# A graph network's message passing on one Trainium2 core: steps of eight tiles without loops, node spans of 32, and stores moved into the counting stage

## The chip, the cores and the metric

The kernel runs on one core of a Trainium2 chip as one program. The core has TensorE (PE, matmuls, with its weight loads PEld), VectorE (DVE), ScalarE (ACT), GpSimd (POOL) and SyncE (SP, which here only issues transfers). The time is the device time of the execution in microseconds, and the median of the runs counts.

## The reference

A graph has 3125 nodes with 96 features and 100,000 edges `src -> dst`, sorted by `dst`; each edge has four attributes. Four layers follow one another, each on `relu(layernorm(x))` and added to x: ten hops of a propagation, a softmax-weighted neighbour sum, message passing with an edge MLP, and two graph convolutions. Cut to the layer that the change is mostly about:

```python
def mlp(h, W, b, gamma, beta):
    h = relu(h @ W + b)
    mu = mean(h, axis=0); var = mean(square(h - mu), axis=0)
    return gamma * (h - mu) * rsqrt(var + EPS) + beta

node_feat = mlp(x, W_node, b_node, g_node, beta_node)             # 3125 x 96
edge_feat = mlp(edge_attr, W_edge, b_edge, g_edge, beta_edge)     # 100000 x 96
message = concatenate([x[src], x[dst], edge_feat], axis=1)        # 100000 x 288
message = mlp(message, W_msg, b_msg, g_msg, beta_msg)             # 100000 x 96
x = x + segment_sum(message, dst, num_segments=3125) + node_feat
```

The other layers need only, for each pair of nodes, how many edges join them: the kernel builds that table of counts once, as a dense matrix of 25 x 25 blocks of 128 x 128, and multiplies with it.

## The kernel before, in words

The stages run one after another, with a barrier between them. `setup` loads the indices, finds which windows of nodes each batch of edges touches, and splits attributes and edge weights into bf16 parts that are stored to HBM (`attr_parts`, `w_edge`); the `dst` of each step's edges is stored as 16 copies of a row (`dst_row`, L227). `count_edges` builds the counts by matmuls of one-hot matrices; beside them it runs the edge MLP once over all edges for its mean and variance. `propagate` does the ten hops, `gen_conv` the second layer. `prepare_messages` computes for each node what it gives to a message as source (`p_rows`, in HBM, for gathers) and as destination (`q`, kept in SBUF as three bf16 parts), and `pass_messages` does the rest; `finish_messages` normalizes; `gcn_first` and `gcn_second` follow.

In `pass_messages` (stage L1210 to L1480) the 784 tiles of 128 edges go in 196 steps of four (`STEP_TILES = 4`), in groups of 14 steps, the middle groups in a hardware loop. For each step:

- SP loads the attributes (L1248) and the `dst` row, broadcast to 128 partitions (L1253).
- POOL gathers the four tiles' rows of `p_rows` (L1276) into one of seven slots of `z`. A slot is free when the step seven before it has been squared (ACT) and summed (PE).
- PE multiplies the attributes with the edge weights (L1404), ACT rectifies (L1360), PE multiplies that with `w_part` (L1412, fp32).
- For each block of 128 nodes that the step's `dst` fall in (a "visit"; 220 in all) DVE makes a turned one-hot (L1288) and copies the block's `q` (L1290), and PE adds the destination's part (L1420, three products per tile).
- DVE adds the gathered rows (L1297), ACT rectifies (L1368) and squares (L1372), DVE adds the squares (L1316).
- For each visit again, DVE makes the one-hot of nodes (L1306, L1309), and PE sums the messages by node into a block of PSUM (L1436). PSUM holds all 25 blocks to the end of the stage.
- PE runs matmuls with zeros (L1393), two ahead of each step's sums and one behind, which add nothing to the sums.

How many visits a step has isn't known when the program is built. The engines read it from a table (L1187, `TENSOR_LOAD`), and the visits are hardware loops with registers as bounds: L1284 and L1303 on DVE, L1416 and L1430 on PE. Order within an engine is the order of the code; between engines it is set by semaphores, for instance

```python
pool.wait_ge(squared, s - SLOTS + 1)
pool.wait_ge(summed, s - SLOTS + 1)
```

ahead of a slot's next gathers.

## Time and profile before

| | us |
|---|---|
| median of 3 runs (3156.49 to 3165.76) | 3164.98 |
| the profiled execution | 3195.45 |
| its span, first to last instruction | 3193.7 |
| setup | 0 to 72 |
| counting, with the edge MLP's statistics | 75 to 649 |
| degrees, first layer norm | 649 to 682 |
| ten hops | 682 to 1218 |
| second layer | 1218 to 1390 |
| preparing messages | 1390 to 1488 |
| passing messages | 1488 to 2950 |
| finish, two convolutions | 2950 to 3193 |

The profile is of one execution; its own time is about 1% above the median, so what is read from it is compared with 3195.45 and carried over to the median at the end. A share of busy time over the whole span (PE 77%, DVE 45%, POOL 28%, ACT 26%) mixes stages with different limits, so the rows below are read by stage. "Idle before" is an engine's idle time directly ahead of an instruction, and the name behind the arrow is what ended it; `issue` is a wait for nothing that the profile shows. Rows with a `q` behind the engine (SPq, PEldq) are of its sequencer.

### The profile page before, as it was taken

The numbers are of one execution on the slowest core, as the hardware profiler recorded it, in microseconds if no ns is written. First come the engines' busy times: TensorE is split into PE (matmuls) and PEld (weight loads), VectorE is DVE, ScalarE is ACT, GpSimd is POOL, SyncE is SP. The second block draws the span as 40 slices with busy tenths as digits, with TensorE's granted clock in tenths as the row PEclk, the third lists the DMA queues.
The fourth block names the chain that finished last, engine by engine and source line by source line (L and its number), as shares of the span: only waits on it lengthen the run. The fifth ranks groups of instructions, "written<-read, shape, count | busy, mean of one in ns | idle before, by whom it ended". The sixth has DMA issues, their size and how long they took to land. (4 is left out here: it accounts for less than half of the span.)

```text
span 3193.7 us, 70454 instructions
## 1 busy us (share of the span) xinstructions
PE 2446.3 (77%) x18850; PEld 1853.2 (58%) x18851; DVE 1451.4 (45%) x3266; ACT 829.0 (26%) x1637; POOL 897.1 (28%) x1115
## 2 busy tenths in 40 slices
PE   0777777779999994965788778788777777777479
PEld 0333444479999993533555556556556655555357
DVE  4967766654444445453333333333333333333642
ACT  1585566521111111111222222222122212122110
POOL 2311211100000000002555555555544555552000
PEclk9989878779999996976677766776776666767799
DMA  5111111100000033001122112111111111111000
GB/s 172 31 46 44 48 55 54 60 27 2 2 2 2 2 131 143 1 10 31 50 58 56 50 51 55 52 52 51 49 48 47 50 45 48 47 49 29 2 1 16
DMA packets 92732, 141.30 MB, mean 44 GB/s; under 512 B 28596, under 2 KB 70916, under 8 KB 92526
## 3 DMA queue, kind: packets, MB, share of 16 engines
q1 hardware_dynamic: 67438, 100.16, 9.2%
q0 software_dynamic: 25088, 38.59, 5.1%
q8 instruction: 106, 1.74, 0.2%
q14 instruction: 100, 0.82, 0.1%
HBM read 105.31 MB, written 33.35 MB: 43 GB/s over the span
## 5 line engine op out<-in xcount | busy, mean ns | idle before, releaser
L1276 POOL DMA_INDIRECT e_z<-p_rows,rows x784 | 767.6, 979 | 653.1 <-issue 270.4
L844 PE MATMUL ps_hop<-y,counts 128*128 128x192 f16 x6250 | 525.1, 247 | 22.4 <-DVEq L768 11.1
L844 PEld LDWEIGHTS ps_hop<-y,counts 128*128 128x128 f16 x6250 | 520.0, 98 | 27.3 <-DVE y L796 11.3
L1436 PE MATMUL ps_e_seg<-e_z,e_hot 128*128 128x96 f32 x1760 | 352.1, 361 | 238.4 <-DVE e_hot L1309 144.2
L1436 PEld LDWEIGHTS ps_e_seg<-e_z,e_hot 128*128 128x128 f32 x1760 | 328.7, 269 | 346.9 <-issue 339.9
L553 PE MATMUL ps_counts<-hot_w,hot_p 128*128 x1196 | 295.9, 380 | 127.2 <-DVE hot_p L527 78.9
L527 DVE TENSOR_TENSOR hot_w<-iota_w,places_now 128x1600 f16<-128x1600 f16 x300 | 297.1, 990 | 205.7 <-PE ps_counts L553 167.4
L1368 ACT ACTIVATE e_z<-e_z 128x384 f32<-128x384 f32 x196 | 102.4, 523 | 1068.1 <-DVE e_z L1297 829.0
L1412 PE MATMUL ps_e_z<-w_part,e_u 96*128 96x96 f32 x1568 | 316.5, 365 | 4.1 <-issue 3.7
L1412 PEld LDWEIGHTS ps_e_z<-w_part,e_u 96*128 96x128 f32 x1568 | 275.5, 264 | 67.9 <-issue 67.3
L1393 PE MATMUL ps_e_seg<-e_zeros,ident_h 128*128 128x512 f16 x608 | 273.5, 516 | 17.8 <-issue 16.8
L553 PEld LDWEIGHTS ps_counts<-hot_w,hot_p 128*128 x1196 | 120.2, 104 | 266.5 <-issue 221.2
L1420 PE MATMUL ps_e_z<-e_q_now,e_hot_t 128*128 x2640 | 222.7, 249 | 48.4 <-issue 40.0
L1288 DVE TENSOR_SCALAR e_hot_t<-e_dst_rows,block_node 128x512 f16 x220 | 80.1, 364 | 369.7 <-issue 310.0
L1420 PEld LDWEIGHTS ps_e_z<-e_q_now,e_hot_t 128*128 x2640 | 203.4, 126 | 65.6 <-issue 60.3
L494 POOL TENSOR_TENSOR places_now<-places,origins (+1 forms) x302 | 110.2, 365 | 458.7 <-DVE hot_p L527 265.9
L1267 POOL MEMSET e_attr<- 39x1024 bf16 x1 | 0.9, 945 | 844.2 <-POOLq L1001 844.2
L1306 DVE TENSOR_SCALAR e_place<-dst_h,block_neg 128x4 f32 (+1 forms) x220 | 53.4, 243 | 348.4 <-PE ps_e_seg L1436 142.4
L826 ACT ACTIVATE y<-wide 128x96 f32 x250 | 70.7, 283 | 465.3 <-DVE wide L789 465.3
L1297 DVE TENSOR_TENSOR e_z<-ps_e_z,e_z 128x384 f32<-128x384 f32 x196 | 109.3, 558 | 169.9 <-remote 117.3
L1309 DVE TENSOR_TENSOR e_hot<-iota_p,e_place 128x512 f32<-128x512 f16 x220 | 152.6, 694 | 9.3 <-DVE e_place L1306 1.4
L617 ACT ACTIVATE attr_split<-ps_counts 128x400 f16<-128x400 f32 x200 | 100.6, 503 | 193.5 <-PE ps_counts L546 193.2
(307 smaller groups left out, 2635.4 us busy)
## 6 DMA issues: line engine op xcount, KB each, us to landing
e_dst_rows<-dst_row SPq DMA_DIRECT2D x196, 128.0 KB
count_rows<-attr_split SPq DMA_DIRECT2D x25, 800.0 KB, 3.7
counts<-count_rows SPq DMA_DIRECT2D x25, 800.0 KB, 6.8
e_z<-p_rows,rows POOLq DMA_INDIRECT x784
attr_parts<-attr_split SPq DMA_DIRECT2D x9, 784.0 KB, 8.9
e_attr<-attr_parts SPq DMA_DIRECT2D x196, 36.0 KB
attr<-attr_parts SPq DMA_DIRECT2D x50, 140.6 KB
dst_row<-counts SPq DMA_DIRECT2D x16, 196.0 KB
```

The lines of the kernel that those rows point to most:

```text
L494: nc.gpsimd.tensor_tensor(now[:, bass.ds(i & 3, 1), :, :, :].rearrange("p a j c t -> p (a j) c t"), k.places[:, bass.ds(tile, BATCH), :].u ...
L527: made = nc.vector.tensor_tensor(hot[:, s, :, :].rearrange("p j (e t) -> p j e t", t=2), iota_w[:, 0:n].rearrange("p (e t) -> p e t", t=2) ...
L553: mm = pe.matmul(ps[:, j % 2, 0:WIDE], hot_p[:, bass.ds(i & 1, 1), t, :].rearrange("p a s -> p (a s)"), hot_w[:, bass.ds(i & 1, 1), t, :]. ...
L844: mm = pe.matmul(ps[:, r, 0:2 * D], k.counts[:, m, b, :], y[:, odd, b, :], start=b == 0, stop=b == NB - 1)
L1276: nc.gpsimd.indirect_dma_start(z[:, s % SLOTS, j, :], None, k.p_rows, bass.IndirectOffsetOnAxis(k.rows[:, t:t + 1], 0)) \
L1297: nc.vector.tensor_tensor(z[:, q % SLOTS, :, :], ps_z[:, q % 2, 0:STEP_TILES * D] .rearrange("p (j f) -> p j f", j=STEP_TILES), z[:, q % S ...
L1309: nc.vector.tensor_tensor(hot[:, :, :], k.iota_p[:, :].unsqueeze(1).broadcast_to([P, STEP_TILES, P]), place[:, :].unsqueeze(2).broadcast_t ...
L1368: nc.scalar.activation(z[:, q % SLOTS, :, :], z[:, q % SLOTS, :, :], ACT.Relu).then_inc(z_relu, 1)
L1393: mm = pe.matmul(ps_seg[:, (m % SEG_BANKS) * BANK:(m % SEG_BANKS + 1) * BANK], k.ident_h[:, :], zeros[:, 0:1].broadcast_to([P, BANK]), sta ...
L1412: pe.matmul(ps_z[:, q % 2, j * D:(j + 1) * D], u[:, q % 2, j * P:(j + 1) * P], k.w_part[:, :], start=j == 0, stop=False, skip_group_check= ...
L1420: mm = pe.matmul(ps_z[:, q % 2, j * D:(j + 1) * D], hot_t[:, bass.ds(x & 1, 1), j * P:(j + 1) * P].rearrange("p a e -> p (a e)"), q_now[:, ...
L1436: mm = pe.matmul(to, hot[:, j, :], z[:, q % SLOTS, j, :], start=False, stop=False, skip_group_check=True)
```

## The change

- A step has eight tiles; there are 98, written out without a hardware loop. `z` has four slots of eight tiles (32 tiles; before 28).
- The destination's part is no longer a product of its own. The edge MLP's output has 96 rows, a matmul takes 128: the 32 others now hold a one-hot of a span of 32 nodes, and the weights below `w_part` hold these nodes' rows of `q` (fp32, from a new HBM table `q_rows`). A step has four spans, each for two tiles (256 edges), which begin at the lowest `dst` of their edges. SP reads where they begin from a table (`lows`) and loads four times 32 rows.
- The sums are made over the 128 nodes from the step's lowest on, in one bank of PSUM per step; DVE adds them with two masks to two blocks of `seg`, now in SBUF. The matmuls with zeros are gone.
- An edge outside its span or its step's 128 nodes gets row 0 of `p_rows` (a very low value, so that it counts for nothing) and is done in a loop at the end, by spans. The number of the loop's rounds is held at one at least.
- `z`, the one-hots, the rectified edges and the squares lie in five of the 25 count blocks, which are read again from HBM in `finish_messages`.
- The stores of `attr_parts`, `w_edge` and `dst_row` are issued at the start of `count_edges`, by SP and ACT, and no longer in `setup`. `setup` computes the new tables on DVE, `propagate` spreads them and makes the masks, mostly on POOL.

**DVE, a step of the message stage.** The names: `e_z` is the step's messages, `e_sq_sum` the sum of squares, `e_hot` the one-hot of nodes; after, `counts` stands for all that lies in the lent blocks, and `seg` is the node sums. Before, from one add of rows to the next:

```order
573 L1297 TENSOR_TENSOR e_z<-ps_e_z,e_z 128x384 [waits e_rows_in6,e_q_done]
574 L1303 UNCONDITIONAL_BRANCH
575 L1303 ISA
576 L1306 REGISTER_ALU [waits e_seg_done]
577 L1306 ISA x3
578 L1306 TENSOR_SCALAR e_place<-dst_h,block_neg 128x4
579 L1309 TENSOR_TENSOR e_hot<-iota_p,e_place 128x512 [waits e_placed]
580 L1303 REGISTER_ALU
581 L1303 COMPARE_AND_BRANCH
582 L1316 TENSOR_TENSOR e_sq_sum<-e_sq_sum,e_z_sq 128x384 [waits e_sq_added,e_squared]
583 L1187 TENSOR_LOAD visit_tabs
584 L1284 ISA
```

and after, one whole step:

```order
407 L1382 TENSOR_TENSOR counts<-ps_e_z,counts 128x768 [waits e_rows_in2,e_z_done]
408 L1394 TENSOR_LOAD lows
409 L1394 ISA x2
410 L1399 ISA [waits e_seg_added,e_seg_done]
411 L1399 SCALAR_TENSOR_TENSOR seg<-ps_e_seg,part_masks,seg 128x96
412 L1399 ISA
413 L1399 SCALAR_TENSOR_TENSOR seg<-ps_e_seg,part_masks,seg 128x96
414 L1375 TENSOR_TENSOR counts<-iota_p,place_h 128x1024 [waits e_seg_done]
415 L1388 TENSOR_TENSOR e_sq_sum<-e_sq_sum,counts 128x768 [waits e_sq_added,e_squared]
416 L1367 TENSOR_TENSOR counts<-e_dst_rows,span_node 32x1024 [waits e_z_done,e_fed_in2]
```

The branches are gone, the operations are twice as wide, and the two masked additions (L1399) have come in.

**PE, a step of the message stage.** `ps_e_z` takes the messages, `ps_e_seg` the node sums, `ps_e_u` the edge MLP. Before, from the zero matmul behind one step's sums to the first product of a visit:

```order
1588 L1430 COMPARE_AND_BRANCH
1589 L1393 MATMUL ps_e_seg<-e_zeros,ident_h 128x512
1590 L1404 MATMUL ps_e_u<-e_attr,w_edge 96x512 [waits e_attr_in1,e_u_ready]
1591 L1412 MATMUL ps_e_z<-w_part,e_u 128x96 [waits e_z_added,e_u_ready]
1592 L1412 MATMUL ps_e_z<-w_part,e_u 128x96 x3
1593 L1187 TENSOR_LOAD visit_tabs
1594 L1416 ISA
1595 L1416 UNCONDITIONAL_BRANCH
1596 L1416 ISA
1597 L1420 REGISTER_ALU [waits e_q_copied]
1598 L1420 ISA
1599 L1420 MATMUL ps_e_z<-e_q_now,e_hot_t 128x96
```

and after, a whole step:

```order
1528 L1510 MATMUL ps_e_z<-e_w_q,counts 128x96 [waits e_z_added,e_turned,e_u_ready]
1529 L1510 MATMUL ps_e_z<-e_w_q,counts 128x96 x7
1530 L1498 MATMUL ps_e_u<-e_attr,w_edge 96x512 [waits e_u_ready,e_fed_in0]
1531 L1498 MATMUL ps_e_u<-e_attr,w_edge 96x512
1532 L1521 MATMUL ps_e_seg<-counts 128x96 [waits e_z_relu,e_hot_ready]
1533 L1521 MATMUL ps_e_seg<-counts 128x96 x7
```

Only matmuls are left, in three runs, each behind one group of waits.

**POOL, the gathers.** Before:

```order
164 L1267 MEMSET e_attr 39x1024
165 L1268 MEMSET e_zeros 128x2
166 L1276 DMA e_z<-p_rows,rows 128x96 x28
167 L1276 DMA e_z<-p_rows,rows 128x96 [waits e_summed,e_squared]
168 L1276 DMA e_z<-p_rows,rows 128x96 x3
169 L1276 DMA e_z<-p_rows,rows 128x96 [waits e_summed,e_squared]
```

and after:

```order
185 L1344 MEMSET e_attr 39x3072
186 L1341 DMA counts<-p_rows,rows 128x96 x32
187 L1341 DMA counts<-p_rows,rows 128x96 [waits e_seg_done,e_squared]
188 L1341 DMA counts<-p_rows,rows 128x96 x7
189 L1341 DMA counts<-p_rows,rows 128x96 [waits e_seg_done,e_squared]
```

POOL gathers eight tiles between two waits, and is four steps of eight ahead.

The diff, cut to its core:

```diff
-STEP_TILES = 4
+STEP_TILES = 8
...
+Q_TILES = 2
+Q_SPANS = STEP_TILES // Q_TILES
+Q_WIDE = P - D
+SLOTS = 4
+FED = 3
...
-            sp.wait_ge(step_row, 1)
-            for copy in range(COPIES):
-                sp.dma_start(k.dst_row[:, copy, :].rearrange("(p a) e -> p a e", a=2),
-                             step_h[0:HALF, :].rearrange("p (a e) -> p a e", a=2)).then_inc(k.row_stored, 16)
...
+            step(nc.vector.scalar_tensor_tensor(step_r[0:STEPS, :], step_f[0:STEPS, :], float(N), step_f[0:STEPS, :],
+                                                ALU.is_lt, ALU.mult))
+            nc.vector.tensor_reduce(high_q[:, :], step_r[0:STEPS, :].rearrange("p (w e) -> p w e", w=Q_SPANS), AX.X, ALU.max)
...
+            for j in range(3):
+                for i in range(3):
+                    sp.dma_start(k.attr_parts[(3 * j + i) * DE:(3 * j + i + 1) * DE, :]
+                                 .rearrange("r (p e) -> p r e", p=P), k.attr_split[:, i, :, :]).then_inc(k.parts_stored, 16)
...
+            act.dma_start(k.lows_row, k.lows_i[:, :]).then_inc(k.lows_stored, 16)
+            for copy in range(COPIES):
+                act.dma_start(k.dst_row[:, copy, :], k.step_h[0:STEPS, :]).then_inc(k.row_stored, 16)
             act.wait_ge(k.parts_stored, 16 * 9)
+            act.wait_ge(k.lows_stored, 16)
+            act.wait_ge(k.row_stored, 16 * COPIES)
...
+                sp.wait_ge(mix_out, (g + 1) * RING)
+                sp.dma_start(k.q_rows[g * RING * P:(g + 1) * RING * P, :].rearrange("(b p) d -> p b d", p=P),
+                             k.seg[:, g * RING:(g + 1) * RING, :]).then_inc(q_stored, 16)
...
-                q = k.q[:, m, :, :]
-                step(nc.vector.tensor_tensor(rest[:, :], ps_w[:, m % 2, D:2 * D], q[:, 0, :], ALU.subtract))
-                step(nc.vector.tensor_copy(q[:, 1, :], rest[:, :]))
-                ins = nc.vector.tensor_tensor(q[:, 2, :], rest[:, :], q[:, 1, :], ALU.subtract)
-                ins.then_inc(mix_out, 1)
-                dve.wait_ge(mix_out, m + 1)
+                nc.vector.tensor_copy(k.seg[:, m, :], ps_w[:, m % 2, D:2 * D]).then_inc(mix_out, 1)
...
+            def feed(fed, s, lows):
+                sp.dma_start(attr[0:PRODUCTS, fed, :], k.attr_parts[:, bass.ds(s * STEP, STEP)]).then_inc(fed_in[fed], 16)
+                sp.dma_start(dst_rows[D:P, fed, :], k.dst_row[bass.ds(s, 1), :, :].rearrange("a c e -> (a c) e").unsqueeze(1)
+                             .broadcast_to([COPIES, Q_WIDE // COPIES, STEP])).then_inc(fed_in[fed], 16)
+                for n, low in enumerate(lows):
+                    sp.dma_start(w_q[D:P, fed, n, :], k.q_rows[bass.ds(low, Q_WIDE), :]).then_inc(fed_in[fed], 16)
+            sp.wait_ge(pool_made, 1)
+            for s in range(STEPS):
+                lows = [sp.value_load(k.lows[0:1, s, n:n + 1], min_val=0, max_val=NP - Q_WIDE) for n in range(Q_SPANS)]
+                if s >= FED:
+                    sp.wait_ge(z_done, s - FED + 1)
...
+            def gather(slot, j, rows):
+                nc.gpsimd.indirect_dma_start(z[:, slot, j, :], None, k.p_rows, bass.IndirectOffsetOnAxis(rows, 0)) \
+                    .then_inc(rows_in[slot], 16)
+
+            nc.gpsimd.memset(attr[:, :, :], 1.0).then_inc(pool_made, 1)
             for s in range(STEPS):
                 if s >= SLOTS:
 
                     pool.wait_ge(squared, s - SLOTS + 1)
-                    pool.wait_ge(summed, s - SLOTS + 1)
+                    pool.wait_ge(seg_done, s - SLOTS + 1)
                 for j in range(STEP_TILES):
                     t = s * STEP_TILES + j
-                    nc.gpsimd.indirect_dma_start(z[:, s % SLOTS, j, :], None, k.p_rows,
-                                                 bass.IndirectOffsetOnAxis(k.rows[:, t:t + 1], 0)) \
-                        .then_inc(rows_in[s % SLOTS], 16)
+                    gather(s % SLOTS, j, k.rows[:, t:t + 1])
...
+            with pool.Fori(0, rest_visits(pool, k)) as x:
+                pool.wait_ge(rest_made, x + 1)
+                nc.gpsimd.tensor_tensor(rest_turn[:, :], rest_rows[:, :], rest_rows[:, :], ALU.add).then_inc(pool_made, 1)
+                for j in range(STEP_TILES):
+                    gather(0, j, rest_rows[:, j:j + 1])
...
+            def turned_hot(s, two, fed, uses, nodes):
+                dve.wait_ge(fed_in[fed], FEED * uses)
+                if not isinstance(s, int) or s >= 2:
+                    dve.wait_ge(z_done, s - 1)
+                nc.vector.tensor_tensor(u_hot[D:P, two, :].rearrange("p (n e) -> p n e", n=Q_SPANS),
+                                        dst_rows[D:P, fed, :].rearrange("p (n e) -> p n e", n=Q_SPANS),
+                                        nodes, ALU.is_equal).then_inc(turned, 1)
+            def hots(s, two, places):
+                if not isinstance(s, int) or s >= 2:
+                    dve.wait_ge(seg_done, s - 1)
+                nc.vector.tensor_tensor(hot[:, two, :, :], k.iota_p[:, :].unsqueeze(1).broadcast_to([P, STEP_TILES, P]),
+                                        places.unsqueeze(2).broadcast_to([P, STEP_TILES, P]), ALU.is_equal) \
+                    .then_inc(hot_ready, 1)
+            def add_rows(s, two, slot, uses):
+                dve.wait_ge(z_done, s + 1)
+                dve.wait_ge(rows_in[slot], ROWS * uses)
+                nc.vector.tensor_tensor(halves(z[:, slot, :, :]), ps_z[:, two, :, 0:HALF_BANK], halves(z[:, slot, :, :]),
+                                        ALU.add).then_inc(z_added, 1)
+            def add_squares(s):
+                dve.wait_ge(squared, s + 1)
+                dve.wait_ge(sq_added, s + 1)
+                nc.vector.tensor_tensor(sq_sum[:, :, :], sq_sum[:, :, :], z_sq[:, :, :], ALU.add).then_inc(sq_added, 1)
+            def block_sum(b):
+                return k.seg[:, bass.ds(b, 1), :].rearrange("p a f -> p (a f)")
+            def add_sums(s):
+                b = dve.value_load(k.lows[0:1, s, LOW_BLOCK:LOW_BLOCK + 1], min_val=0, max_val=NB - 1)
+                sums = [block_sum(b + n) for n in range(2)]
+                dve.wait_ge(seg_done, s + 1)
+                dve.wait_ge(seg_added, s + 1)
+                for n in range(2):
+                    added = nc.vector.scalar_tensor_tensor(sums[n], ps_s[:, s % 2, 0:D], k.part_masks[:, n, s:s + 1],
+                                                           sums[n], ALU.mult, ALU.add)
+                added.then_inc(seg_added, 1)
...
+            turned_hot(0, 0, 0, 1, step_nodes(0))
+            hots(0, 0, step_places(0))
+            turned_hot(1, 1, 1, 1, step_nodes(1))
+            for s in range(STEPS):
+                add_rows(s, s % 2, s % SLOTS, s // SLOTS + 1)
+                if s:
+                    add_sums(s - 1)
+                if s + 1 < STEPS:
+                    hots(s + 1, (s + 1) % 2, step_places(s + 1))
+                add_squares(s)
+                if s + 2 < STEPS:
+                    turned_hot(s + 2, s % 2, (s + 2) % FED, (s + 2) // FED + 1, step_nodes(s + 2))
+            add_sums(STEPS - 1)
...
+                    turned_hot(x + STEPS, 0, 0, x + (FED_USES + 1), nodes)
+                    hots(x + STEPS, 0, places)
+                    add_rows(x + STEPS, 0, 0, x + (SLOT_USES + 1))
+                    add_squares(x + STEPS)
+                    mine = block_sum(v >> 2)
+                    dve.wait_ge(seg_done, x + (STEPS + 1))
+                    nc.vector.tensor_tensor(mine, mine, ps_s[:, 0, 0:D], ALU.add) \
+                        .then_inc(seg_added, 1)
...
+            def edge_mlp(s, two):
+                act.wait_ge(u_done, s + 1)
+                if not isinstance(s, int) or s >= 2:
+                    act.wait_ge(z_done, s - 1)
+                nc.scalar.activation(u_hot[0:D, two, :].rearrange("p (h e) -> p h e", h=2), ps_u[:, :, :], ACT.Relu) \
+                    .then_inc(u_ready, 1)
+            def rectified(s, slot):
+                act.wait_ge(z_added, s + 1)
+                nc.scalar.activation(z[:, slot, :, :], z[:, slot, :, :], ACT.Relu).then_inc(z_relu, 1)
+                act.wait_ge(z_relu, s + 1)
+                act.wait_ge(sq_added, s + 1)
+                nc.scalar.activation(z_sq[:, :, :], z[:, slot, :, :], ACT.Square).then_inc(squared, 1)
...
+            def edges(s, fed, uses):
+                pe.wait_ge(fed_in[fed], FEED * uses)
+                if not isinstance(s, int) or s:
+                    pe.wait_ge(u_ready, s)
+                for h in range(2):
+                    mm = pe.matmul(ps_u[:, h, :], k.w_edge[:, :], attr[:, fed, h * BANK:(h + 1) * BANK],
+                                   start=True, stop=True)
+                mm.then_inc(u_done, 1)
+            def messages(s, two, fed):
+                pe.wait_ge(u_ready, s + 1)
+                pe.wait_ge(turned, s + 1)
+                if not isinstance(s, int) or s >= 2:
+                    pe.wait_ge(z_added, s - 1)
                 for j in range(STEP_TILES):
...
+                    at = j % (STEP_TILES // 2) * D
+                    mm = pe.matmul(ps_z[:, two, j // (STEP_TILES // 2), at:at + D], u_hot[:, two, j * P:(j + 1) * P],
+                                   w_q[:, fed, j // Q_TILES, :], start=True, stop=True, skip_group_check=True)
+                mm.then_inc(z_done, 1)
+            def sums(s, two, slot):
+                pe.wait_ge(hot_ready, s + 1)
+                if not isinstance(s, int) or s >= 2:
+                    pe.wait_ge(seg_added, s)
+                pe.wait_ge(z_relu, s + 1)
+                for j in range(STEP_TILES):
+                    mm = pe.matmul(ps_s[:, two, 0:D], hot[:, two, j, :], z[:, slot, j, :], start=j == 0,
+                                   stop=j == STEP_TILES - 1)
+                mm.then_inc(seg_done, 1)
+            edges(0, 0, 1)
+            pe.wait_ge(w_set, 1)
+            messages(0, 0, 0)
+            edges(1, 1, 1)
+            for s in range(STEPS):
+                if s + 1 < STEPS:
+                    messages(s + 1, (s + 1) % 2, (s + 1) % FED)
+                if s + 2 < STEPS:
+                    edges(s + 2, (s + 2) % FED, (s + 2) // FED + 1)
+                sums(s, s % 2, s % SLOTS)
+            with pe.Fori(0, rest_visits(pe, k)) as x:
+                edges(x + STEPS, 0, x + (FED_USES + 1))
+                messages(x + STEPS, 0, 0)
+                sums(x + STEPS, 0, 0)
...
+            for m in range(LENT, NB):
+                sp.dma_start(k.counts[:, m, :, :].rearrange("p b s -> p (b s)"), k.count_rows[m, :, :]) \
+                    .then_inc(k.counts_in[m % RING], 16)
```

## Rows read from the trace of the kernel before

**Rows 1.** Busy time by stretch: us, busy (x count) per engine, PEclk, DMA.

```profile
0.00:75.00 75.00, 4.43 (x23) 3.25 (x24) 38.66 (x53) 8.52 (x6) 18.37 (x27) 1.00 0.48 159
...
1488.00:2950.00 1462.00, 1130.27 (x6778) 843.85 (x6778) 526.24 (x1277) 310.37 (x593) 768.57 (x786) 0.70 0.19 50
```

**Rows 2.** Lines of the message stage, each shape: busy us, mean ns | idle before.

```profile
L1276 POOL DMA_INDIRECT e_z<-p_rows,rows x784 | 767.6, 979 | 653.1 <-issue 270.4 <-PE ps_e_seg L1393 219.6 <-ACT e_z_sq L1372 90.5
L1436 PE MATMUL ps_e_seg<-e_z,e_hot 128*128 128x96 f32 x1760 | 352.1, 361 | 238.4 <-DVE e_hot L1309 144.2 <-issue 93.6
...
L1412 PE MATMUL ps_e_z<-w_part,e_u 96*128 96x96 f32 x1568 | 316.5, 365 | 4.1 <-issue 3.7
...
L1393 PE MATMUL ps_e_seg<-e_zeros,ident_h 128*128 128x512 f16 x608 | 273.5, 516 | 17.8 <-issue 16.8
...
L1309 DVE TENSOR_TENSOR e_hot<-iota_p,e_place 128x512 f32<-128x512 f16 x220 | 152.6, 694 | 9.3 <-DVE e_place L1306 1.4 <-issue 0.6
...
L1316 DVE TENSOR_TENSOR e_sq_sum<-e_sq_sum,e_z_sq 128x384 f32<-128x384 f32 x196 | 108.5, 554 | 18.0 <-issue 17.9
...
L1343 DVE TENSOR_TENSOR sq<-e_sq_sum 128x96 f32<-128x96 f32 x1 | 0.3, 259 | 0.0
```

**Rows 3.** The gathers' line: ns min/median/max, first and last start.

```profile
L1276 POOL DMA_INDIRECT e_z<-p_rows,rows x784: 942/947/1463, 1489.1 to 2908.7; - x196
```

**Rows 4.** POOL in order of time, around the first 28 gathers: start, us.

```profile
1487.97 0.94 POOL L1267 MEMSET e_attr<- 39x1024 bf16 x1 [844.24 <-POOLq L1001]
...
1489.13 1.12 POOL L1276 DMA_INDIRECT e_z<-p_rows,rows  x1 [0.18 <-issue]
...
1523.14 0.95 POOL L1276 DMA_INDIRECT e_z<-p_rows,rows  x1 [0.30 <-issue]
1534.72 1.22 POOL L1276 DMA_INDIRECT e_z<-p_rows,rows  x1 [10.63 <-ACT e_z_sq L1372]
```

**Rows 5.** PE in order of time, two steps at different granted clocks.

```profile
1540.26 0.97 PEld L1412 LDWEIGHTS ps_e_z<-w_part,e_u 96*128 96x128 f32 x8 [0.23 <-issue]
...
2206.99 0.66 PE L1404 MATMUL ps_e_u<-e_attr,w_edge 39*96 39x512 bf16 x1
2207.58 1.78 PEld L1412 LDWEIGHTS ps_e_z<-w_part,e_u 96*128 96x128 f32 x8 [0.44 <-issue]
```

**Rows 6.** POOL and DVE in order of time: two gathers and what ran beside them.

```profile
1541.49 0.94 POOL L1276 DMA_INDIRECT e_z<-p_rows,rows  x1 [1.79 <-ACT e_z_sq L1372]
1541.60 0.69 DVE L1309 TENSOR_TENSOR e_hot<-iota_p,e_place 128x512 f32<-128x512 f16 x1
...
2211.57 1.23 POOL L1276 DMA_INDIRECT e_z<-p_rows,rows  x1 [0.30 <-issue]
2211.89 0.55 DVE L1316 TENSOR_TENSOR e_sq_sum<-e_sq_sum,e_z_sq 128x384 f32<-128x384 f32 x1
```

**Rows 7.** Sequencers: table loads and asserts (ns min/median/max), one DMA issue in the stage.

```profile
L1187 SPq TENSOR_LOAD <-visit_tabs x194: 4/440/728, 1499.5 to 2923.4; - x194
...
L1436 PEldq SEQ_ASSERT  x880: 3/18/726, 1531.3 to 2945.9; - x176
...
2209.76 0.55 SPq L1253 DMA_DIRECT2D e_dst_rows<-dst_row  x1
```

**Rows 8.** Setup and the start of counting, in order of time: SP, DVE, POOL, ACT.

```profile
37.05 14.44 SPq L227 DMA_DIRECT2D dst_row<-counts  x16
...
46.24 0.56 DVE L360 CAST window_tabs<-ps_row 1x400 int32<-1x400 f32 x1
...
59.13 12.49 SPq L238 DMA_DIRECT2D attr_parts<-attr_split  x9
...
72.22 1.76 POOL L480 MEMSET attr<- 39x2000 bf16 x1 [39.12 <-POOLq L148]
...
101.27 0.50 ACT L617 ACTIVATE attr_split<-ps_counts 128x400 f16<-128x400 f32 x1 [27.85 <-PE ps_counts L546]
```

520 lines of the change are left out of this document (226 added, 294 removed).

## Prediction

> **What bounds the kernel now.** I read the page first, then the busy time by stage, then the message stage by line, and last single steps of it. The stages show where the time is: message passing lasts 1462.0 us of the 3193.7 us span, and setup ends at about 72 us [rows 1]. In the message stage PE is busy 1130 us, at a granted clock of 0.70, POOL 769 and DVE 526. No engine is full, so the stage is bound by how its steps hand over: 196 steps of four tiles take 1462/196 = 7.46 us each. By line [rows 2], 273.5 us of PE is matmuls with zeros (L1393, 608 of 516 ns), which do no work. A lone gather on POOL takes 947 ns in the median, 942 at least [rows 3]. Where nothing holds POOL, the first 28 gathers run from 1489.13 to 1523.14: 34.01/27 = 1.26 us from one to the next, of which 0.30 is issue. The next comes at 1534.72, after 10.63 us of waiting for squares [rows 4]. So POOL needs 784 x 1.25 = 980 us, 482 less than it gets now. That difference is the most that a better hand-over can give while the 784 gathers stay, and they stay.
>
> The slow part of the hand-over is in the loops. Register work in them is mostly short, but has long cases: the assert of L1436 has a median of 18 ns and a longest of 726, the table load of L1187 on SP 440 and 728 [rows 7]. Each visit in a loop on PE and DVE goes through several of them.
>
> **The change, part by part.** The sum is made against the profiled execution, 3195.45 us. It is 30.5 us above the median of the three runs (3164.98), so I scale the end by 3164.98/3195.45 = 0.9905.
>
> *Message stage, engine by engine, for one of the 98 steps of eight tiles.* A DVE operation of 128 x 96 takes 259 ns and one of 384 columns 554 [rows 2]: 1.02 ns a column. So 768 columns cost 0.95 us and 1024 cost 1.21. DVE after: add of rows 0.95, square sums 0.95, two one-hot operations 2 x 1.21, two masked sums 2 x 0.26, a table load of about 0.4; together 5.2 us. PE after: 16 fp32 passes (eight tiles) for the messages, 16 for the sums, two matmuls of L1404's kind. Eight such passes (PEld) took 1.78 us at the low clock and 0.97 at the full one, L1404 0.66 at the low [rows 5]. Low: 4 x 1.78 + 2 x 0.66 = 8.4 us. High, with L1404's at the same ratio: about 4.6. The zero matmuls (273.5 us) and the three-way bf16 products are gone. SP after: six DMAs and four table loads; one DMA issue in this stage took 0.55, so 6 x 0.55 + 4 x 0.44 = 5.1 us; by the slower issue of setup (12.49/9 = 1.39) 10.1 us [rows 7, 8]. POOL after: 8 x 1.25 = 10.0 us. POOL is the longest in every clock, and with four slots of eight tiles (32 gathers, against 28 before) it is 40 us ahead at most. So POOL paces: this is where the stage's time comes from.
>
> *Do the gathers stay at 1.25?* A gather took 1.23 us beside a square add of 0.55 (two fp32 inputs in SBUF): 0.28 more than the median for 0.55 us beside. Beside the one-hot of 0.69, whose first input is a broadcast table, one took 0.94 [rows 6]. The square adds grow to 0.95 each, and POOL now gathers without pause, so each of the 98 meets gathers: 0.28/0.55 x 0.95 = 0.48, and a part falls in the 0.30 gaps; I take 0.41, 40 us. Bounds: nothing, and the whole add, 98 x 0.95 = 93 us. I take 980 + 2 for the stage's first, long ones + 40 = 1022 us.
>
> The Trainium skill (*SBUF — State Buffer*, "SBUF: two separate sides") says that a DVE operation with two SBUF inputs and a GpSimd one that reads SBUF take a shared port pair in turn, the later fully blocked. The row with the square add agrees with the direction (0.28 of 0.55), the one with the one-hot, which has two SBUF inputs as well, doesn't. Taken at its word the rule gives the first rival below.
>
> *Around the gathers.* A memset of 39 x 1024 took 0.94 us and one of 39 x 2000 1.76 [rows 4, 8]; 39 x 3072 gives 2.7, with the first issue 2.9 us. The last step behind the last gather: landing about 2 (an estimate; none is shown), add 0.95, rectify about 0.8, sums 4 x 0.9, masked add 0.6: 8 us. Then the loop for what lies outside the spans. In the drawn edges the widest half-quarter of a step (256 sorted edges) covers 17 nodes, the span is 32; the widest step covers 64, and 128 are allowed. So nothing is left over, but the counts are held at one at least, so one visit is run, in series: table loads 3, eight gathers 10, landing 2, adds and rectify 2.7, sums 3.6, last additions and feed 2.7: 24 us (bounds 12 and 35). And 1.5 for the end of the square sums. Message stage: 2.9 + 1022 + 8 + 24 + 1.5 = 1058 us, against 1462: **-404**.
>
> *Setup and counting.* Now SP issues 16 row copies for 14.44 us from 37.05, then weights, then nine stores for 12.49 us until 71.6, while DVE's last operation starts at 46.24; the counting stage begins with POOL's memset at 72.22 [rows 8]. After, no transfer is issued there, so DVE ends it. DVE gets one more operation of 1024 columns (1.2) and some 17 more small ones at 0.26 (4.4), a part of them beneath its waits: the stage begins at about 52. The stores are then issued in the counting stage, on SP and ACT. What waits for them: ACT's first eviction, now 29.05 us after the memset (101.27 - 72.22), so 81 after. ACT issues 17 DMAs first, 17 x 0.90 = 15.3 us, so until 67, and waits for both groups; if the bytes of setup and these went one behind another they would be done 36 us after 52, at 88. A delay of 0 to 7 us at the first window, and the ring of windows lets PE go on meanwhile; I take 1. Net **-19** (bounds -24 and 0).
>
> *The rest.* Propagation gets three DVE operations of 784 columns (0.9 each) beside PE's degree sums and a POOL part that nothing in the ten hops waits for: **+1** (0 to +6). Preparation has one copy where three dependent operations stood, where PE's matmuls pace: **-0.5** (-10 to +2, as 25 stores more go to q_rows). In the finish the five lent count blocks are read again, 800 KB each; they are first needed at block 20 of 25 of the next stage: 0 (up to +10).
>
> Sum: 3195.45 - 404 - 19 + 1 - 0.5 = 2773 us profiled, x 0.9905 = 2747. I say **2745**. Own range: stretch of gathers 0 to 93, rest loop 12 to 35, setup 0 to -24, the small ones to +10; not all at one end: 2700 to 2790.
>
> **Rivals.** *A, DVE blocks the gathers with all its SBUF operations.* The one-hots too have two SBUF inputs, 2.42 us a step: 98 x 2.42 x 0.28/0.55 = 121 us more, 2773 + 121 = 2894, x 0.9905 = 2866. For it: one of the two has another form than before (32 partitions, both inputs new tables). Against it: the 0.94 us gather under a one-hot [rows 6]. 0.10.
>
> *B, the feed paces.* SP at 1.39 per issue and 0.73 per load needs 6 x 1.39 + 4 x 0.73 = 11.3 us, with waits some 12: 98 x 12 = 1176 instead of 1022, +154, so 2927 x 0.9905 = 2899. For it: queues on which DMAs of a few partitions cost 1.39. Against it: the 0.55 of the same kind of issue inside this stage [rows 7], and three buffers. 0.09.
>
> *C, slower than before: slow instructions stay and are multiplied.* If the 0.7 us cases [rows 7] come from POOL's gathers beside them and not from the loops, they hit straight code too, and POOL now never pauses. PE issues 74 instructions a step (34 weight loads, 34 matmuls, six waits). At the mean clock the step's work is 6.2 us. The change loses from (1462 + 18 - 36)/98 = 14.7 us a step, which 12 slow ones make (16%). With a quarter slow: 6.2 + 18.5 x 0.7 = 19 us a step, a stage of 1898, and 3195 - 1462 + 1898 - 18 = 3613, x 0.99 = 3580. For it: they are dense while gathers run. Against it: the eight passes of L1412 at 0.97 us [rows 5], straight code, ran with gathers about. 0.03. On the loops the Trainium skill (*Runtime: NRT & Kernel Launch*, "Instruction fetch mechanics") says that a taken branch out of the two fetched pages stalls the engine; that would put the long cases on loops, and no row here separates it from the gathers.
>
> *D, it doesn't do what it says:* wide spans would add visits of about 20 us each in series. The drawn indices leave none; 0.02, at a time near 2790.
>
> **How the numbers follow.** Forecast 0.76, A 0.10, B 0.09, C 0.03, D 0.02. The predicted time is the forecast's. The range must take A in, and most of a gentler low end (no stretch, a faster loop): 2695 to 2870, which leaves out B, C and a tenth of the forecast. A measurement here tells about 0.3% from no change. All but C are faster by far; of B's and A's worst mixtures I give 0.01 to no change. Faster 0.96, same 0.01, slower 0.03.
>
> **What would show it.** Right: POOL busy some 1000 of a message stage of about 1058 us, its idle mostly issue and not ACT or PE; eight gathers in 10.0 to 10.5 us; PE's mean clock below 0.8 without effect; the first operation of counting at about 52. Wrong: POOL's waits named for squares or sums in the middle of the stage (B or C); gathers of 1.2 us or more beside L1375 or L1367 (A); PE's idle as issue in straight code (C); the first eviction later than 88.

## The result and the profile after

The changed kernel takes 2923.31 us (median of 4, 2912.51 to 2938.55) beside 3164.43 us before (4 runs, 3156.49 to 3165.76): ratio 0.9248, 95% interval 0.9218 to 0.9277. It is 7.5% faster. I had said 2745 us, with 2695 to 2870 as the range: the sign was right, the size was not. The profiled execution has a span of 2910.8 us, 283.0 less than the profile of before. That profile is of a slow one among the executions of before (3195.45 us), so the differences below are some 40 us larger than those of the medians. Traced on one chip (c2 and c1 below) the spans differ by 230.9 us and the message stages by 211.4 (1430.0 and 1218.6 us).

By stages, read from the first instruction of each in the two traces:

| from, to | before | after | difference | forecast |
|---|---|---|---|---|
| start, first hop product | 681.9 | 659.5 | -22.4 | -18 |
| ten hops, to the second layer's products | 571.0 | 571.3 | +0.3 | 0 |
| those, to the message stage's first memset | 235.2 | 217.9 | -17.3 | -0.5 |
| message stage | 1461.9 | 1217.3 | -244.6 | -404 |
| finish to end | 243.8 | 244.8 | +1.0 | 0 |

So the miss in the profile is one stage, 1217 us where 1058 were forecast; the other stages give back 20 of these 159 us. Against the medians comes a second one: I had multiplied by 0.9905, since the profile of before lay 1% above its median, but here the profiled execution (2912.51 us) is the fastest of the four. Of the 178 us between 2745 and 2923, 139.5 are in the profile and 39 in that factor. The busy time of its gathering part (columns as in rows 1, here from the first gather to the last):

```profile
1451.00:2628.00 1177.00, 703.09 (x3286) 606.03 (x3287) 461.41 (x581) 258.05 (x291) 837.76 (x785) 0.60 0.22 49
```

and by line (columns as in rows 2; `counts` are the lent blocks), where L1341 answers to L1276, L1521 to L1436, L1510 to L1412:

```profile
L1341 POOL DMA_INDIRECT counts<-p_rows,rows x784 | 837.9, 1069 | 339.2 <-issue 245.5 <-remote 90.1 <-PE ps_e_seg L1521 3.6
L1521 PE MATMUL ps_e_seg<-counts 128*128 128x96 f32 x1584 | 325.7, 370 | 166.5 <-issue 150.6 <-ACT counts L1473 11.1 <-DVE seg L1399 4.7
L1510 PE MATMUL ps_e_z<-e_w_q,counts 128*128 128x96 f32 x1584 | 323.5, 389 | 307.4 <-issue 201.3 <-ACT counts L1468 106.1
...
L1367 DVE TENSOR_TENSOR counts<-e_dst_rows,span_node 32x1024 f32<-32x1024 f16 x98 | 119.7, 1222 | 10.7 <-DMA e_w_q<-q_rows 7.0 <-issue 0.7
L1468 ACT ACTIVATE counts<-ps_e_u 96x1024 f32<-96x1024 f32 x99 | 101.0, 1020 | 823.0 <-remote 563.1 <-issue 179.8 <-PE ps_e_u L1498 80.1
```

Operations cost what was forecast: 1.22 us for 1024 columns on DVE [rows 2]. But the gathers have a mean of 1069 ns instead of 979 [rows 2], and POOL, which I had made the pace, waits besides: 90.1 us for something that ended elsewhere. From the first gather to the last it is 1176.0 us, where 1022 were forecast. What stands behind the gathers (to the end of the stage) took 38.6 us, with 33.5 forecast. The 154 us between 1176 and 1022 are 94 us of waits for slots (90.1 + 3.6; none were forecast), 54 of the gathers' own length (837.9 where 784 x 0.947 + 42 = 784 were forecast) and the rest issue.

PE's and SP's rows tell more than POOL's. SyncE's table loads and the register work around them in straight code (ns min/median/max, as in rows 7):

```profile
L1324 SPq TENSOR_LOAD <-lows x392: 2/269/1400, 1451.3 to 2605.5; - x196
L1324 SPq FUSED_REGOPS  x392: 2/147/1402, 1451.8 to 2605.8; - x196
L1324 SPq SEQ_ASSERT  x392: 2/18/1397, 1452.0 to 2606.0; - x196
```

Medians are short, and the longest are twice those of the loops before [rows 7]: 307 of the 1999 such instructions of SyncE took over 0.6 us. Nothing here is a branch. And in order of time (start, us; `remote` is a semaphore whose sender the profile doesn't name), a step and a half:

```profile
2411.67 2.02 PE L1510 MATMUL ps_e_z<-e_w_q,counts 128*128 128x96 f32 x16
...
2413.62 0.63 PE L1498 MATMUL ps_e_u<-e_attr,w_edge 39*96 39x512 bf16 x2
...
2424.33 0.96 DVE L1382 TENSOR_TENSOR counts<-ps_e_z,counts 128x768 f32<-128x768 f32 x1 [5.97 <-remote]
...
2426.39 8.42 SPq L1320 DMA_DIRECT2D e_w_q<-q_rows  x4
2426.46 1.02 ACT L1468 ACTIVATE counts<-ps_e_u 96x1024 f32<-96x1024 f32 x1 [15.33 <-remote]
...
2427.53 3.73 PE L1510 MATMUL ps_e_z<-e_w_q,counts 128*128 128x96 f32 x16 [9.32 <-issue]
...
2432.75 0.29 PEld L1521 LDWEIGHTS ps_e_seg<-counts 128*128 128x128 f32 x1 [1.33 <-issue]
2433.45 0.32 PE L1521 MATMUL ps_e_seg<-counts 128*128 128x96 f32 x1 [0.82 <-issue]
2434.15 0.29 PEld L1521 LDWEIGHTS ps_e_seg<-counts 128*128 128x128 f32 x1 [1.11 <-issue]
2434.85 0.32 PE L1521 MATMUL ps_e_seg<-counts 128*128 128x96 f32 x1 [1.08 <-issue]
...
2436.40 1.88 POOL L1341 DMA_INDIRECT counts<-p_rows,rows  x1 [3.48 <-remote]
```

The 16 message passes were through by 2413.7 in the records, and the add that needs them (L1382, whose gathers had landed) starts at 2424.33; the edge products were through at 2414.25, and ACT's L1468, which needs those, starts at 2426.46. TensorE's word that it has finished comes 10.6 and 12.2 us late. At 2432.75 its instructions follow each other at 0.70 us exactly. I call both a hold-up below. Of the 99 message products 90 have the update of their semaphore on record; 60 of these come more than 1 us after the product's end, 486 us in all, and the latest 22.6 us. POOL waits 3.5 us at nearly every third step: 32 times more than 1 us, 109 us in all with the issue, mostly after 24 gathers and never after more than 40. One more thing in this trace bears on what follows. Each transfer ends with 16 updates of a semaphore (16 packets of 4 bytes), and of the 12672 that the gathers made the trace holds 2926, although the packets of a gather were mostly through 2.1 to 3.2 us after its start. What the profile calls `remote` can therefore be an update of this core that isn't on record.

Setup and counting came as forecast in sum:

```profile
51.25 1.76 POOL L512 MEMSET attr<- 39x2000 bf16 x1 [18.11 <-POOLq L162]
...
58.23 23.83 ACTq L647 DMA_DIRECT2D dst_row<-counts  x11
...
88.15 0.50 ACT L656 ACTIVATE attr_split<-ps_counts 128x400 f16<-128x400 f32 x1 [35.69 <-DMA dst_row<-counts]
```

The stage begins at 51.3 (52 forecast) and the first eviction is at 88.15, just past the 81 to 88 of the forecast: it waits for `dst_row`, and 11 of its issues took 23.83 us, 2.2 each, where SyncE had needed 0.90 [rows 8]. The ring of windows hid it.

### The profile page after: what moved, and what is told of

The parts are those of the page before. It is cut to its first block and busy times, and to the rows that moved or that the text cites. A ratio compares the mean times of both kernels' runs of the same rounds, so it can differ in the third digit from the quotient of the medians.

```text
span 2910.8 us, 52183 instructions
## 1 busy us (share of the span) xinstructions
PE 2011.6 (69%) x15441; PEld 1617.6 (56%) x15442; DVE 1396.7 (48%) x2559; ACT 779.5 (27%) x1318; POOL 1002.3 (34%) x1142
## 3 DMA queue, kind: packets, MB, share of 16 engines
q0 software_dynamic: 25344, 38.98, 6.7%
## 5 line engine op out<-in xcount | busy, mean ns | idle before, releaser
L1341 POOL DMA_INDIRECT counts<-p_rows,rows x784 | 837.9, 1069 | 339.2 <-issue 245.5
L1510 PE MATMUL ps_e_z<-e_w_q,counts 128*128 128x96 f32 x1584 | 323.5, 389 | 307.4 <-issue 201.3
L1510 PEld LDWEIGHTS ps_e_z<-e_w_q,counts 128*128 128x128 f32 x1584 | 308.7, 299 | 341.7 <-issue 229.0
L1521 PE MATMUL ps_e_seg<-counts 128*128 128x96 f32 x1584 | 325.7, 370 | 166.5 <-issue 150.6
L1521 PEld LDWEIGHTS ps_e_seg<-counts 128*128 128x128 f32 x1584 | 296.4, 277 | 217.7 <-issue 216.4
L1468 ACT ACTIVATE counts<-ps_e_u 96x1024 f32<-96x1024 f32 x99 | 101.0, 1020 | 823.0 <-remote 563.1
L1399 DVE SCALAR_TENSOR_TENSOR seg<-ps_e_seg,part_masks,seg 128x96 f32 x196 | 52.8, 311 | 511.5 <-remote 490.2
L1382 DVE TENSOR_TENSOR counts<-ps_e_z,counts 128x768 f32<-128x768 f32 x99 | 94.8, 957 | 199.6 <-remote 166.1
L1071 PE MATMUL ps_gen<-y,counts 128*128 128x384 f16 x625 | 115.1, 336 | 44.5 <-DVE y L994 44.5
L559 DVE TENSOR_TENSOR hot_p<-iota_w,places_now 128x512 f16<-128x512 f16 x300 | 127.4, 425 | 0.0
L1367 DVE TENSOR_TENSOR counts<-e_dst_rows,span_node 32x1024 f32<-32x1024 f16 x98 | 119.7, 1222 | 10.7 <-DMA e_w_q<-q_rows 7.0
```

What stands on the lines that cost most here:

```text
L559: made = nc.vector.tensor_tensor(hot[:, s, :, :].rearrange("p j (e t) -> p j e t", t=2), iota_w[:, 0:n].rearrange("p (e t) -> p e t", t=2) ...
L1071: mm = pe.matmul(ps[:, m % RING, 0:4 * D], k.counts[:, m, b, :], y[:, b, :], start=b == 0, stop=b == NB - 1)
L1341: nc.gpsimd.indirect_dma_start(z[:, slot, j, :], None, k.p_rows, bass.IndirectOffsetOnAxis(rows, 0)) \
L1367: nc.vector.tensor_tensor(u_hot[D:P, two, :].rearrange("p (n e) -> p n e", n=Q_SPANS), dst_rows[D:P, fed, :].rearrange("p (n e) -> p n e", ...
L1382: nc.vector.tensor_tensor(halves(z[:, slot, :, :]), ps_z[:, two, :, 0:HALF_BANK], halves(z[:, slot, :, :]), ALU.add).then_inc(z_added, 1)
L1468: nc.scalar.activation(u_hot[0:D, two, :].rearrange("p (h e) -> p h e", h=2), ps_u[:, :, :], ACT.Relu) \
```

## The experiments

All were run beside the kernel before. The time of each is that of one execution, except c1 (median of 4). The time of the kernel before differs between the groups of runs, and the kinds of chip below go by it: 3160 to 3199 us is the first kind, 2823 the second or other. The groups came to four chips: e1 to e4, e5 to e8, c1 to c4, and g1 to h2. "Stage" is from the message stage's first memset to the next stage's first product where the text gives no other bounds.

| run | edit | kernel before on that chip | time |
|---|---|---|---|
| e1 | no gathers after step 4 | 3198.51 | 2332.79 |
| e2 | half the gathers | 3198.51 | 2442.41 |
| e3 | sums in fewer, longer matmuls | 3198.51 | 2914.31 |
| e4 | squares added over 96 columns | 3198.51 | 2932.18 |
| e5 | one-hots with an fp32 input | 2822.67 | 2747.37 |
| e6 | six slots | 2822.67 | 2747.49 |
| e7 | gathers of 64 rows | 2822.67 | 2716.42 |
| e8 | one node load per step | 2822.67 | 2740.86 |
| c1 | the changed kernel, timed again | 3160.90 | 2924.86 |
| c2 | the kernel before, traced again | 3160.90 | 3156.22 |
| c3 | e6 again | 3160.90 | 2942.22 |
| c4 | e5 again | 3160.90 | 2921.63 |
| g1 | gathers first, steps after | 3163.72 | 3390.83 |
| g2 | gathers and steps, not coupled | 3163.72 | 3316.19 |
| g3 | gathers of 48 columns | 3163.72 | 2919.97 |
| g4 | e7 again | 3163.72 | 2919.38 |
| h1 | plain loads by GpSimd | 3197.90 | 2320.02 |
| h2 | plain loads by SyncE | 3197.90 | 3241.90 |

**Without gathers.**

```diff
-            for s in range(STEPS):
+            for s in range(SLOTS):
```

> Only the first 32 gathers of the message stage are made; the later 94 steps add to old rows of their slot (the output is not the reference's). In the changed kernel a step takes 12.0 us on average. Theory 1 (slow instructions): while gathers run, TensorE and SyncE finish instructions up to 0.7 us apart, and the chain over TensorE paces; without gathers these phases are gone and a step takes 8.5 to 10 us at the low clock, 5.5 to 7 at the high one, with hardly any register instruction of 0.6 to 0.8 us left on SyncE. Theory 2 (shared port): the stretched gathers pace; without them the step is also under 10 us, but SyncE's slow instructions have nothing to do with gathers and stay as many. Theory 3 (chain alone): hand-overs and the low clock make 12 us by themselves; the step stays at 12 us and the time the same within 1%.

```profile
1475.00:2075.00 600.00, 489.68 (x3330) 433.21 (x3330) 460.93 (x588) 263.16 (x293) 28.35 (x30) 0.87 0.15 34
```

The stage is 631.4 us, the steps take 6.1 us, and 13 of SyncE's 1999 instructions are slow, all while the first 32 gathers run or just behind them. Theory 3 (the chain needs 12 us by itself) is out: the chain can run twice as fast. So is the part of theory 2 by which SyncE's slow instructions stay. TensorE's granted clock is 0.87 here, against 0.60 of the changed kernel.

**Half the gathers** (`for j in range(STEP_TILES if s < SLOTS else STEP_TILES // 2)`).

> From the fifth step on only four of eight tiles are gathered (the output is not the reference's); GpSimd needs 5 us per step instead of 10. Theory 1: the slow phases go with the share of time in which gathers run; the step falls to 9.5 to 10.5 us, and the slow register instructions on SyncE become fewer but stay. Theory 2: the step is what the chain takes without stretched gathers, about 8.5 to 9.5 us, and no slow phases matter. Theory 3: 12 us.

From the first gather to the last of the 98 steps 697 us, 7.1 us per step, and 98 slow instructions of SyncE. That is under what all three theories gave, but on the side of the first two: the hold-up goes with the time in which gathers run.

**Fewer, longer sums.**

```diff
-                for j in range(STEP_TILES):
-                    mm = pe.matmul(ps_s[:, two, 0:D], hot[:, two, j, :], z[:, slot, j, :], start=j == 0,
-                                   stop=j == STEP_TILES - 1)
+                for j in range(2):
+                    mm = pe.matmul(ps_s[:, two, 0:4 * D], hot[:, two, j, :],
+                                   z[:, slot, 4 * j:4 * j + 4, :].rearrange("p j f -> p (j f)"), start=j == 0, stop=j == 1)
```

> The node sums are two fp32 matmuls of 384 columns instead of eight of 96: the same number of columns on TensorE, 8 records of instructions instead of 32 (the output is not the reference's). Theory 1: fewer instructions to be held up, so the step gets shorter, 11.0 to 11.5 us, where GpSimd with its stretched gathers (about 11.0) becomes the pace: 50 to 100 us off the stage. Theories 2 and 3: TensorE has as many columns as before and GpSimd as many gathers, so the stage changes by less than 15 us.

1172 us from the first gather to the last instead of 1176: my theory 1 failed in the form in which it was put. A quarter of the instructions in the sums saves nothing, so the 12.0 us are not simply a count of TensorE's instructions times a delay.

**Small additions of squares** (`sq_sum[:, 0:1, :]` for `sq_sum[:, :, :]`).

> The addition of squares on VectorE takes 96 columns instead of 768 (the output is not the reference's), so 0.26 us instead of 0.95, with two SBUF inputs either way. Theory 2 (and my own 40 us of stretch, measured as 96): gathers lose most of their extra time, mean from 1069 ns to under 985, and if they pace, the stage gets 70 to 95 us shorter. Theory 1: the gathers get shorter as well, but the chain over TensorE paces, GpSimd waits longer for its slots, and the stage gets 0 to 30 us shorter. If the gathers keep 1069 ns, it is not this addition that stretches them but the one-hots.

The gathers' mean falls to 1045 only, and their part of the stage is 1188 us, 12 longer. So neither is the stretch the pace, nor is it mostly this addition that stretches. In the trace of the changed kernel a fit of the 784 gathers' durations on their overlap with DVE's operations gives 0.61 us more per us beside the node one-hot (L1367), whichever other operations are in the fit; the place one-hot (L1375) comes out at 0.37 or 0.63, the square add (L1388) at 0.32 or 0.13, depending on whether the sums' addition (L1399) is in it. My choice of the square add from [rows 6] as the only cause was wrong here.

**Another kind of chip.** The next four ran on a chip on which the kernel before takes 2822.67 us.

```diff
-                nc.vector.tensor_tensor(hot[:, two, :, :], k.iota_p[:, :].unsqueeze(1).broadcast_to([P, STEP_TILES, P]),
+                nc.vector.tensor_tensor(hot[:, two, :, :], iota_f[:, :].unsqueeze(1).broadcast_to([P, STEP_TILES, P]),
...
-                return k.span_node[D:P, s, :].unsqueeze(2).broadcast_to([Q_WIDE, Q_SPANS, Q_TILES * P])
+                return span_f[D:P, s, :].unsqueeze(2).broadcast_to([Q_WIDE, Q_SPANS, Q_TILES * P])
```

> Both one-hots get one fp32 input (a table of node numbers kept in fp32) where both were f16 in the changed kernel; nothing else differs. In the trace of the changed kernel a gather is longer by 0.6 us per us beside a one-hot, and before the change, with one fp32 and one f16 input, by 0.07. Theory F (two f16 inputs take what the gather needs): the gathers' mean falls from 1069 to under 990 ns. If GpSimd paces, the stage (1176 us from first to last gather) falls by the whole 70 to 90 us; if the late completions on TensorE pace, the gathers get shorter and GpSimd's waits for slots get longer, and the stage falls by less than 30. Theory G (their width of 1024 columns or the broadcast does it): the mean stays over 1050 ns.

```diff
-SLOTS = 4
+SLOTS = 6
-LENT = NB - RING
+LENT = NB - RING - 1
```

> Six slots of eight tiles instead of four (a sixth count block is lent for it and read again in the finish). Theory J (the late completions are uneven, GpSimd runs out of slots every third step and waits 94 us in all): the waits fall under 30 us and the stage by 60 to 90 us, to the 11.0 us per step of the stretched gathers. Theory K (the chain over TensorE needs 12 us per step on average while gathers run): the waits stay and the stage changes by less than 20 us.

```diff
-                nc.gpsimd.indirect_dma_start(z[:, slot, j, :], None, k.p_rows, bass.IndirectOffsetOnAxis(rows, 0)) \
+                nc.gpsimd.indirect_dma_start(z[0:n, slot, j, :], None, k.p_rows, bass.IndirectOffsetOnAxis(rows[0:n], 0)) \
```

> From the fifth step on each gather brings 64 rows instead of 128 (the output is not the reference's); there are as many gathers. Theory 1a (the DMA traffic of the gathers holds up the completions on other engines): about half of the delays go, the step falls towards the gathers' own pace. Theory 1b (GpSimd's making of the gathers does it): if a gather takes nearly as long on GpSimd with 64 rows (over 900 ns), delays and stage stay; if it gets shorter with its rows, both get shorter and the run cannot tell 1a from 1b.

```diff
-                for n, low in enumerate(lows):
+                for n, low in list(enumerate(lows))[0:1]:
```

> Of the four loads of 32 node rows per step one is left, and one of four table loads, so that SyncE has three DMAs per step instead of six (the output is not the reference's). Theory B (the feed paces, rival B of the prediction): the step falls by 0.5 us or more. Theory K or GpSimd as the pace: the stage changes by less than 15 us. If the small loads and not the gathers fill what the completions need, the delays on TensorE fall as well.

All four are at 2716 to 2747 us and none of SyncE's instructions is slow. With six slots all 99 message products have their update within 0.02 us of their end, and 12634 of the gathers' 12672 updates are on record. The gathers of the run with six slots (ns min/median/max), and the busy time beside them:

```profile
L1341 POOL DMA_INDIRECT counts<-p_rows,rows x784: 940/944/1862, 1457.2 to 2462.0; - x196
```

```profile
1457.00:2462.00 1005.00, 642.53 (x3316) 584.71 (x3316) 463.52 (x585) 252.81 (x292) 766.20 (x783) 0.69 0.25 57
```

1005 us for the gathers with 979 ns each and no wait for a slot: the picture of the forecast (1022), a stage of 1046.7 us (1058) and a time of 2747 (2745). The four edits differ, and only the two that cut work from the transfers moved something: 64 rows make a gather 932 ns, and one node load 974. With the trace's 98 waits of DVE for gathers that land (526.4 us), POOL paces here. But since the kernel before was 340 us and more faster as well, none of the four expectations was tested in its first half.

**The two kernels again, and two of the edits, on a chip of the first kind.**

> The changed kernel once more, timed beside the kernel before on one chip. The kernel before took 3156 to 3199 us on the chips of the first runs and 2823 on the chip of the last four, where no register instruction of SyncE took 0.6 to 0.8 us and GpSimd never waited for a slot. Theory C (the held-up completions are a state of the chip, not of the kernel): where the kernel before takes about 2820, the changed one takes 2740 to 2760, ratio 0.97 to 0.98, with a message stage of 1045 to 1060 us; where it takes 3160 to 3200, about 2920 and 1215. Theory S (the edits of the last four runs all happened to remove the delays): the changed kernel takes 2900 or more wherever it runs.

> The kernel before, for its trace on this chip. Theory C: on a chip where it takes about 2820 us, the register instructions in its loops all take under 0.5 us and the message stage is about 1100 us instead of 1462, close to the 980 us of the gathers; on one where it takes over 3150, the loops have their 0.7 us instructions and the stage is 1440 to 1480.

> Six slots instead of four, as in the earlier run, now beside the changed kernel on one chip. On a chip with held-up completions: theory J (uneven delays, more lead bridges them) 60 to 90 us less than the changed kernel; theory K (the chain needs 12 us per step on average) within 20 us of it. On a chip without: the same time as the changed kernel within 5 us, since GpSimd waits for no slot.

> The one-hots with one fp32 input, as in the earlier run, beside the changed kernel on one chip. On a chip with held-up completions: theory F says the gathers' mean falls from 1069 to under 990 ns; if their length there comes with the delays and not with the type of an input, it stays over 1050. On a chip without: the gathers have 979 ns either way and the time is the same within 5 us.

Ratio 0.9234 (0.9201 to 0.9266): theory C holds as far as it was tried (the changed kernel itself didn't run on a chip of the other kind). Theory S is out by the two edits: the same six slots and the same fp32 inputs that took 2747 us take 2942 and 2922 here. Whether it is the chip, or when it was used, can't be told: none was seen in both conditions, and the faster one in one group of runs only. Six slots: from the first gather to the last 1175 us. Theory K, then: more lead bridges nothing where the average is too slow. One fp32 input: mean 1068 ns, so the type of an input isn't what stretches gathers. On the chip of the other kind the same fit on the same code (e5) gave 0.08 us per us beside the node one-hot, here 0.63 to 0.64, with the same input types. The stretch beside that one-hot comes with the hold-up.

**What the gathers do by themselves.**

```diff
+            dve.wait_ge(spare_done, 1)
             turned_hot(0, 0, 0, 1, step_nodes(0))
```

(with the gathers from step 5 on going to two spare buffers of seven tiles, paced by their landing; g2 is the same without this wait).

> The gathers of step 5 on go to two spare buffers of seven tiles, paced by their own landing, and VectorE begins its steps only when all 784 are done; the steps then add to old rows (the output is not the reference's). So gathers and steps run one after the other. On a chip where the kernel before takes over 3150: theory L (the gathers' own traffic allows one per 1.5 us there: 784 x 1.5 = 1176 us, what the stage took with four and with six slots, with and without fp32 tables) expects the gathers alone to take 1176 us. Theory M (gathers and the other engines hold each other up) expects 980 to 1000 us alone, and then steps of 6.1 us as without gathers. On a chip where before takes about 2820, 980 to 1000 us in any case.

> As the run with the gathers first, but the steps run beside the gathers, neither waiting for the other after step 4 (the output is not the reference's). On a chip of the first kind: theory L expects the gathers to end after 1176 us and the steps, 98 of some 6 to 9 us, well before them. Theory M expects both to be slowed: gathers over 1.4 us each while steps run and 1.25 when these are through, steps of 9 us or more, and late completions on TensorE although it waits for no gather. On a chip of the second kind: gathers 1.25 to 1.28 us, steps 6 to 8.5 us.

POOL in order of time, first early, then late, all other engines idle:

```profile
1600.20 0.94 POOL L1357 DMA_INDIRECT e_spare<-p_rows,rows  x1 [0.30 <-issue]
1601.45 0.95 POOL L1357 DMA_INDIRECT e_spare<-p_rows,rows  x1 [0.30 <-issue]
...
1999.79 1.10 POOL L1357 DMA_INDIRECT e_spare<-p_rows,rows  x1 [0.30 <-issue]
2001.19 1.09 POOL L1357 DMA_INDIRECT e_spare<-p_rows,rows  x1 [0.31 <-issue]
```

For 189 gathers one every 1.25 us, and from then to the last one every 1.400 us, twice the 0.70 us of the slow instructions; 1068 us in all. After the last gather the steps take 5.8 us at once.

In g2 the gathers need 1070 us, so the steps beside them hardly slow them. But the steps all but stand still: 13 of the 98 are made in that time, from the third on one every 95.2 us, and as soon as the gathers are through a step takes 5.8 us. One step, with 34 matmuls and 34 weight loads (columns as in rows 1), and TensorE within the next:

```profile
1617.50:1712.70 95.20, 9.99 (x34) 8.39 (x34) 4.72 (x7) 2.59 (x3) 72.35 (x75) 0.50 0.19 41
```

```profile
1727.35 0.29 PEld L1534 LDWEIGHTS ps_e_seg<-counts 128*128 128x128 f32 x1 [1.95 <-issue]
...
1728.75 0.32 PE L1534 MATMUL ps_e_seg<-counts 128*128 128x96 f32 x1 [2.21 <-issue]
...
1730.15 0.29 PEld L1534 LDWEIGHTS ps_e_seg<-counts 128*128 128x128 f32 x1 [2.51 <-issue]
...
1731.55 0.32 PE L1534 MATMUL ps_e_seg<-counts 128*128 128x96 f32 x1 [2.48 <-issue]
```

No engine but GpSimd has work for an eighth of the 95.2 us. Of TensorE's 68 instructions half start within 5 us and most of the others 1.40 us apart, and behind them lies a gap of 44 us; 68 x 1.40 is 95.2, so it looks as if something took all of them at that rate, but that is read from the numbers and not shown. So neither theory is right as put. The gathers alone are limited (L), but to 1.40 us and not at once. The large effect is one-sided (M in part): gathers without a pause hold up the steps sixteenfold. In the coupled kernels a step can only fall so far behind before GpSimd has to wait for a slot, and the two together go at 1.50 us per gather. That the steps catch up in GpSimd's pauses would explain why six slots gain nothing (29 pauses, 115 us, where four have 32 and 109); it is read from these traces and no run tests it.

**Columns and rows** (`z[:, slot, j, 0:D // 2]` from a table of half rows; `z[0:P // 2, slot, j, :]`).

> From step 5 on a gather brings 48 columns of each of the 128 rows, so as many descriptors and half the bytes (the output is not the reference's). On a chip of the first kind, theory N (number of descriptors or of gathers): the stage's 1176 us stay within 20. Theory O (bytes): the stage falls by 100 us or more. On one of the second kind nothing changes (1005 us from first to last gather).

> From step 5 on a gather brings 64 rows, so half the descriptors and half the bytes in as many gathers, as in the earlier run, which fell on a chip of the second kind (932 ns and 968 us from first to last). On a chip of the first kind: if descriptors or bytes set the 1.5 us, the stage falls by 100 us or more towards 970; if the number of gathers sets it, it stays at 1176 within 20.

Both stay: 1180 and 1179 us from the first gather to the last. Bytes, and the number of rows, don't set the 1.50 us; the number of gathers is what is left, and with half of them (e2) the stage did fall. POOL's own time for 64 rows is 903 ns in the median and it waits 135 us instead.

**The same traffic without the index.**

```diff
-                    gather(s % SLOTS, j, k.rows[:, t:t + 1])
+                    nc.gpsimd.dma_start(z[:, s % SLOTS, j, :], k.p_rows[t % NB * P:(t % NB + 1) * P, :]) \
+                        .then_inc(rows_in[s % SLOTS], 16)
```

> Each gather is replaced by a plain load of 128 consecutive rows, issued by GpSimd as before (the output is not the reference's): the same bytes and the same order, but nothing indirect. On a chip where the kernel before takes over 3150: theory Q (transfers that GpSimd writes itself hold up the others) expects late completions on TensorE, slow register instructions on SyncE and a step near 12 us as long as a load takes GpSimd about 1 us; theory R (it is the indirect kind that does it) expects a step under 11 us and few slow instructions on SyncE. On a chip where before takes about 2820 the run tells only what a plain load costs GpSimd.

The queue's row in its page and in that of the changed kernel (packets, MB, share), and then its loads:

```profile
q0 software_dynamic: 25344, 38.98, 7.0%
```

```profile
q0 software_dynamic: 25344, 38.98, 6.7%
```

```profile
L1352 POOL DMA_DIRECT2D counts<-p_rows x784: 534/534/794, 1459.9 to 2028.3; - x196
```

```profile
1460.00:2050.00 590.00, 486.81 (x3334) 429.98 (x3334) 468.44 (x594) 264.92 (x294) 414.26 (x786) 0.88 0.39 98
```

The same 25344 packets with the same 38.98 MB through the same queue, in half the time, and none of SyncE's 1999 instructions over 0.6 us; 12656 of the 12672 semaphore updates are on record. Theory R: it is the indirect kind. Neither the amount of traffic nor the fact that GpSimd issues it holds anything up. Two things go with the indirect kind here and were not separated: the rows lie scattered, and GpSimd works 0.94 us on each instead of 0.53.

> The same plain loads of 128 consecutive rows, issued by SyncE, two steps ahead (the output is not the reference's). SyncE then issues 14 DMAs per step, some 9 us. On a chip of the first kind: theory Q expects the late completions and the slow register instructions to be gone (under 20 us of the latter, as without gathers, where it was 16) and a step of 8.5 to 10 us; theory T (the traffic of eight times 48 KB per step does it, whoever issues it) expects 12 us or more with the delays as before.

3241.9 us, which no theory gave, and no slow instruction: SyncE issues 14 DMAs per step, and a step takes some 15 us because the node rows come late (782.6 us of DVE's waits are for `e_w_q`). The loads by SyncE were 0.47 us apart in a row, so their issue explains 7 us; the rest of the 15 was not followed up. For the question it says the same as h1: no hold-up without indirect gathers.

**What goes along with the hold-up in every trace.** Of the semaphore updates of the loads of `p_rows` the trace holds 13 to 34% in the two kernels and in all edits on chips of the first kind that gather by index (g2 1628, g1 1684, c1 2870 of 12672, e1 214 of 640, c2 4308 of 12544), and over 99.5% in h1, h2 and e5 to e8. So wherever instructions are late, records are lacking as well. Either several updates came as one, or the recording could not take them all. In the second case the recording itself may be what holds the engines up, and since every time here is that of a recorded execution, no run tells how long the kernels take without it.

## Why the prediction was wrong

**The step that failed** is "So POOL paces: this is where the stage's time comes from", with 1022 us for the gathers. They took 1176 us, which is 154 of the stage's 159 us. The sum let the steps run beside the gathers at their own 5.2 to 8.4 us and put GpSimd's waits for slots at nothing. The runs show in its place that indirect gathers hold up the other engines on these chips: without gathers a step takes 5.8 to 6.1 us (e1), beside gathers that never pause 95.2 (g2), and coupled 12.0, with 94 us of waits for slots and 54 us more of the gathers' own length. I had read the 1.25 us from a stretch of 28 gathers in which nothing waited ([rows 4]) and which was over before VectorE's first add of rows (1529.0). g1 shows one more thing that such a stretch hides, the 1.40 us after 189 gathers in a row; but the changed kernel never makes more than 40 without a pause, so that limit isn't the one it met.

**Rival C named the mechanism** and I gave it 0.03. It said that the 0.7 us instructions might come from the gathers and not from the loops, and would then hit straight code. e1 and h1 show the first half (no slow instructions once the indirect gathers are over, or without any), the SyncE rows and the PE rows after show the second. Its price was far too high: with 3.6 us a step of `issue` ahead of L1510 and L1521 (201.3 + 150.6 over 98), and a hold-up that works as a pace and not per instruction (e3), the step is 12.0 us and not 19. I had counted against it the eight passes of L1412 at 0.97 us [rows 5], "straight code, ran with gathers about". But no gather ran then: the passes lie from 1540.26 to 1541.23, and the gather at 1541.49 had been waiting 1.79 us for a slot [rows 6], so since 1539.70. And the hold-up comes in stretches: the steps after have undisturbed passes too, beside gathers (2411.67, 16 in 2.02 us). One undisturbed instance doesn't exclude an effect that comes and goes; the share of instructions at 0.70 us by what ran beside them would have shown it. A rule of the Trainium skill had leaned the same way (*Runtime: NRT & Kernel Launch*, "Instruction fetch mechanics": a taken branch out of the two fetched pages stalls the engine). This case's trace doesn't bear it out as the cause of the 0.7 us: 307 instructions of SyncE outside any branch are slow, and none in the same code with plain loads (h1).

**Rival B** had the time, 12 us a step and 2899, by another way (SyncE's feed). In the trace after DVE's L1367 waits 7 us for node rows, and on the chip of the other kind e8 is 6.5 us under e5; on the first kind e8 wasn't run. So the time of B was met by accident.

**Rival A** (all DVE operations with two SBUF inputs block the gathers, after *SBUF — State Buffer*, "SBUF: two separate sides", of the Trainium skill) is half met: the node one-hot does lengthen the gathers, by 0.61 us per us, on chips of the first kind, and by 0.08 on the other. As far as e4 tests it, it costs nothing in the time: 19 us less of the gathers' own length there became more waiting. GpSimd's extra 96 us over the median seem to take the place of waits. The same instruction with the same operands lies at either value, so the port alone isn't the cause of the larger one; the measurement decides.

**Point by point.** DVE, ACT and PE times per step were right (1.22, 0.95, 3.7 us for 16 passes at the low clock). Setup and counting: -19 forecast, -21 at the start of counting, and -22.4 at the first hop product, with the +1 of propagation in it. The stage's end: 33.5 forecast, 38.6 measured. Preparation: -0.5 forecast, -17.3 measured, outside my bounds (-10 to +2). I had taken TensorE's matmuls as its pace; but these were 733 ns before and 496 after:

```profile
L1154 PE MATMUL ps_w<-w,h_t 97*128 97x288 f32 x50 | 31.5, 733 | 2.2 <-DVE q L1089 1.9
```

```profile
L1235 PE MATMUL ps_w<-w,h_t 97*128 97x288 f32 x50 | 20.5, 496 | 0.5
```

The granted clock was 0.50, the lower of its two levels (1.2 GHz), in these 25 blocks before (1417 to 1454), and 0.86 after (1395 to 1418); with the three dependent DVE operations gone the blocks followed faster, 22 us instead of 37. The pair c2 and c1 gives the same clocks and 16.0 us for the part. That the clock rose because TensorE waited less was not tested by itself.

**Right for another chip.** On the chip without hold-ups the forecast of the stage (1058) and of the time (2745) is met by the two variants that do all of the work (e5, e6), 1047 and 2747. But there the kernel before takes 2823, so the gain is 2.7%, not 13%. The forecast joined the kernel before of one kind of chip with the kernel after of the other.

**What stays open.** Why an indirect gather holds up the instructions of other engines, why it needs a run-up (189 gathers when alone), and what differs between the chips. Whether the recording of the traces has a part in it is the rival that no run tests. Bytes, the number of rows, the number of packets, GpSimd as issuer, slots and input types are excluded as causes of the 1.50 us. The number of TensorE's instructions isn't settled: e3 has a third fewer and is as slow, while the 95.2 us of g2 look like a rate per instruction. No version faster than the changed kernel on chips of the first kind came out of these runs; only the gathers' number is left to cut, and a gather takes one index per partition here.

## What to carry to other kernels

A rate read from a short undisturbed stretch (28 gathers) is no rate for 784 of them: look for the longest run of the operation that the trace has, and say how much longer the new one is. That engines are free of each other has to be read where both work at once; an instance that is to speak against a rival must lie where the rival's cause was at work. Slow register instructions are a symptom with a place of their own; before a change is credited with removing them, count them by what else runs at the same time, not by the code that they stand in. And where the kernel before takes 11 to 12% less on one chip than on another, the gain has to be compared within a chip, since the part that a change removes may exist on one kind only.

## What the runs showed of the hardware

- With indirect gathers running, instructions of SyncE and TensorE follow at 0.70 us in stretches, and TensorE's completions came up to 22.6 us late (changed kernel); with plain loads, in the same code and on one of the same chips, neither was seen (h1). Three of the four chips of these experiments showed it, the fourth in none of its four runs. All executions were recorded ones, and the traces with the hold-up lack 65% and more of the gathers' semaphore updates.
- Beside indirect gathers that never pause, a step of all other engines took 95.2 us, and 5.8 us without gathers (g2).
- Indirect gathers alone go at 1.25 us for 189 and at 1.400 us from then on (g1); a plain load of the same 48 KB through the same queue takes GpSimd 534 ns (h1).
- Half the rows or half the columns leave the pace at 1.50 us per gather where it is held up (g3, g4).
